# The token norm ahead of a quantized feed-forward: scale found after normalizing, steps moved between engines, batch 1's tokens spread over four tiles

## What is computed

```
x = x + attention(layernorm(x), ctx)
x = x + ffn(layernorm(x))            # this second layernorm, and what follows it

layernorm(x)  = (x - mean(x)) / sqrt(var(x) + 1e-5)
bit_linear(x, w, b):
    gamma_x = max(max(|x|), 1e-5);  scale_x = 127 / gamma_x         # per token
    x_dq = clip(round(x * scale_x), -128, 127) / scale_x
    gamma_w = max(mean(|w|), 1e-5)
    w_dq = clip(round(w / gamma_w), -1, 1) * gamma_w
    return x_dq @ w_dq.T + b
ffn(x) = bit_linear(silu(bit_linear(x, gate_w, gate_b)) * bit_linear(x, val_w, val_b), out_w, out_b)
```

## Time and profile before

| | |
|---|---|
| median of 3 runs | 970.87 us (970.19 to 971.57) |
| the profiled execution | 969.66 us, of which the trace's span is 967.6 us |
| PE busy over the span | 876.3 us (91%) |
| DVE / ACT / POOL busy | 834.3 / 528.2 / 556.3 us |
| last head's end to start of feed-forward | about 821 to 836.5 us |
| feed-forward | 836.5 us to the end |

### The profile page before, as it was taken

The page is one execution under the profiler, slowest core; times in us unless marked ns, Lnnn a source line. Parts: engine busy times, 40 slices in busy tenths (PEclk is TensorE's granted clock), DMA queues, the critical chain, the costliest instruction groups (busy, mean ns, idle before and its releaser), DMA issues. The chain is left out here.

```text
span 967.6 us, 15479 instructions
## 1 busy us (share of the span) xinstructions
PE 876.3 (91%) x4290; PEld 672.3 (69%) x4290; DVE 834.3 (86%) x1234; ACT 528.2 (55%) x885; POOL 556.3 (57%) x551
## 2 busy tenths in 40 slices
PE   3556999999999999999999999999999798738996
PEld 2434888878888788878888888888888676313543
DVE  6756899988998999899989988998899778686996
ACT  2315556655655575566656655665566477443332
POOL 5176646465555746574657465646464678664661
PEclk9768999999999999999999999999999998778999
DMA  8000121011101110111011101110210168100000
GB/s 302 0 21 27 55 67 36 27 40 47 46 14 50 46 35 24 39 46 35 24 39 46 35 24 44 50 39 20 66 46 14 34 252 306 52 0 12 22 22 33
DMA packets 25174, 51.73 MB, mean 53 GB/s; under 512 B 5440, under 2 KB 11840, under 8 KB 23872
## 3 DMA queue, kind: packets, MB, share of 16 engines
q1 hardware_dynamic: 24064, 49.36, 15.8%
q10 hardware_dynamic: 1088, 2.10, 0.6%
HBM read 49.35 MB, written 2.10 MB: 53 GB/s over the span
## 5 line engine op out<-in xcount | busy, mean ns | idle before, releaser
L791 POOL TENSOR_TENSOR rot_cos<-rot_cos,rot_sin 128x512 f32<-128x512 f32 x93 | 120.1, 1291 | 147.3 <-DVE rot_sin L985 135.7
L895 ACT ACTIVATE probs<-scores,neg_max 128x1024 f32<-128x1024 f32 x128 | 144.0, 1126 | 74.8 <-DVE neg_max L1011 74.0
L976 DVE TENSOR_TENSOR pt_lo<-banks,pt_hi 128x512 fp32r<-128x512 f32 x256 | 164.3, 683 | 9.8 <-ACT pt_hi L879 7.5
L879 ACT CAST pt_hi<-banks 128x512 fp32r<-128x512 f32 x256 | 138.3, 596 | 54.5 <-PE banks L1154 54.5
L1011 DVE TENSOR_REDUCE neg_max<-scores 128x1 f32<-128x1024 f32 x128 | 155.8, 1218 | 9.9 <-PE scores L1171 9.0
L1154 PE MATMUL banks<-ident,probs 128*128 128x128 f32 x1024 | 134.8, 275 | 10.0 <-PEq L1213 5.4
L1154 PEld LDWEIGHTS banks<-ident,probs 128*128 128x128 f32 x1024 | 119.9, 141 | 28.7 <-issue 5.8
L799 POOL TENSOR_TENSOR rot_lo<-rot_cos,rot_hi 128x512 fp32r<-128x512 f32 x93 | 119.7, 1287 | 7.8
L1006 DVE SCALAR_TENSOR_TENSOR acc<-banks,inv,acc 128x512 f32<-128x512 f32 x128 | 92.6, 747 | 12.9 <-PE banks L1086 10.9
L1086 PE MATMUL banks<-pt_hi,v_hi 128*128 128x512 f32 x256 | 102.9, 402 | 0.9
L1086 PE MATMUL banks<-pt_hi,v_lo 128*128 128x512 f32 x256 | 101.0, 394 | 0.0
(11 more groups left out here) (194 smaller groups left out, 2014.4 us busy)
## 6 DMA issues: line engine op xcount, KB each, us to landing
load<-in_pack SPq DMA_DIRECT2D x15, 320.0 KB, 2.9
raw_chunk<-in_out_w SPq DMA_DIRECT2D x8, 512.0 KB, 3.7
load<-in_pack SPq DMA_DIRECT2D x16, 256.0 KB, 2.7
raw_chunk<-in_gate_w SPq DMA_DIRECT2D x8, 512.0 KB, 3.6
raw_chunk<-in_val_w SPq DMA_DIRECT2D x8, 512.0 KB, 4.3
raw<-in_gate_w SPq DMA_DIRECT2D x4, 1024.0 KB, 5.8
raw<-in_val_w SPq DMA_DIRECT2D x4, 1024.0 KB, 5.1
raw<-in_out_w SPq DMA_DIRECT2D x4, 1024.0 KB, 5.2
```

Of the source, the lines that this page charges most:

```text
L791: nc.gpsimd.tensor_tensor(total, total, rot_sin[:, c, :], ALU.add).then_inc(rot_sum, 1)
L879: nc.scalar.copy(out, src).then_inc(group_hi, 1)
L895: nc.scalar.activation(probs[:, u % 2, :], scores[:, u % 2, :], ACT.Exp, bias=neg_max[:, u:u + 1], accum_out=sums[:, u:u + 1]).then_inc(ex ...
L976: return nc.vector.tensor_tensor(pair[1], src, pair[0].bitcast(F32), ALU.subtract)
```

## The change

- The last head and tiles 0 and 1: `statistics` is one DVE instruction per tile; maximum and minimum of the raw rows are gone. The rows are normalized without the quantization scale (`deviation`, `normalize`), and the largest magnitude is then taken from the normalized rows (`extreme`, one DVE pass per tile); `scales` has four small instructions.
- POOL's `lift` is two passes in place (times scale plus MAGIC; clip from both sides) over one buffer of four tiles, where it was one pass between two buffers of two.
- `take` moves from DVE to ACT. In the last head the transposes go to the `scores` banks.
- In the last head the second norm's steps stand ahead of V1's take-out on ACT and, partly, on DVE; two weight drops move behind them on ACT.
- In the feed-forward four tiles are written out, and batch 1's lifts, transposes and takes are placed in tiles 2 and 3 by three tables. Tiles 0 to 3 wait for their own token tile, the loop (tiles 4 to 7, two turns) for all eight.

```diff
+TOKENS_LIFTED = {(2, 0): 4, (2, 2): 5, (3, 0): 6, (3, 2): 7}
+TOKENS_TURNED = {(2, 7): 4, (3, 2): 5, (3, 5): 6, (3, 7): 7}
+TOKENS_TAKEN = {(3, 0): 4, (3, 1): 5, (3, 2): 6, (3, 3): 7}
...
     def statistics(self, dve, u):
-        nc, tile, one = self.nc, self.t["acc"][:, u, :], slice(u, u + 1)
-        nc.vector.bn_stats(self.stats[:, u, :], tile)
-        nc.vector.tensor_reduce(self.most[:, one], tile, AX, ALU.max)
-        nc.vector.tensor_reduce(self.least[:, one], tile, AX, ALU.min).then_inc(self.seen, 1)
+        self.nc.vector.bn_stats(self.stats[:, u, :], self.t["acc"][:, u, :]).then_inc(self.seen, 1)
...
+    def deviation(self, dve, b):
+        nc, half = self.nc, slice(b * U, (b + 1) * U)
+        rstd = self.rstd[:, half]
+        inverse_deviation(nc, dve, self.var_eps[:, half], self.root[:, half], rstd, self.tmp[:, half], self.root_ready, b + 1,
+                          lambda ins: self.link(dve, ins))
+        nc.vector.scalar_tensor_tensor(out=self.shift[:, half], in0=self.mv[:, half, 0], scalar=-1.0, in1=rstd, op0=ALU.mult,
+                                       op1=ALU.mult).then_inc(self.shift_ready, 1)
+
+    def normalize(self, act, u):
+        act.wait_ge(self.shift_ready, u // U + 1)
+        self.nc.scalar.activation(self.tile(u), self.t["acc"][:, u, :], ACT.Identity, bias=self.shift[:, u:u + 1],
+                                  scale=self.rstd[:, u:u + 1]).then_inc(self.normed_ready, 1)
+
+    def extreme(self, dve, u):
+        dve.wait_ge(self.normed_ready, u + 1)
+        self.nc.vector.tensor_reduce(self.most[:, u:u + 1], self.tile(u), AX, ALU.max,
+                                     apply_absolute_value=True).then_inc(self.most_ready, 1)
...
     def lift(self, pool, u):
-        pool.wait_ge(self.normed_ready, u + 1)
-        self.nc.gpsimd.tensor_scalar(self.lifted[:, u % 2, :], self.normed[:, u % 2, :], MAGIC, MAGIC + 127, ALU.add,
-                                     ALU.min).then_inc(self.lifted_ready, 1)
+        tile = self.tile(u)
+        pool.wait_ge(self.scale_ready, u // U + 1)
+        self.nc.gpsimd.tensor_scalar(tile, tile, self.x_scale[:, u:u + 1], MAGIC, ALU.mult, ALU.add).then_inc(self.lifted, 1)
+        pool.wait_ge(self.lifted, u + 1)
+        self.nc.gpsimd.tensor_scalar(tile, tile, MAGIC + 127, MAGIC - 128, ALU.min, ALU.max).then_inc(self.clipped, 1)
...
-    def take(self, dve, u, src):
-        return self.nc.vector.tensor_scalar(self.t["xt"][:, :, u * P:(u + 1) * P], src.rearrange("p (c s) -> p c s", c=KD),
-                                            MAGIC, -128.0, ALU.subtract, ALU.max)
+    def take(self, act, u, src):
+        act.wait_ge(self.turned, u + 1)
+        self.nc.scalar.activation(self.t["xt"][:, :, u * P:(u + 1) * P], src.rearrange("p (c s) -> p c s", c=KD),
+                                  ACT.Identity, bias=self.t["minus_magic"][:]).then_inc(self.taken, 1)
...
-            tile(Head(0), 0)
-            tile(Head(1), 1)
-            with engine.Fori(0, (NU - 2) // 2) as i:
+            for n in range(U):
+                tile(Head(n), min(n, 2))
+            with engine.Fori(0, (NU - U) // 2) as i:
...
-                if h.i is not None:
-                    pe.wait_ge(x_read, U)
+                if n == 0:
+                    pe.wait_ge(second.taken, h.number + 1 if h.i is None else NU)
...
+                pe.wait_ge(second.taken, u)
+                second.turn(pe, u, ps_x)
...
-                    if before == 1 and n == 1:
-                        second.scales(dve, 1)
-                    if before == 1 and n in (4, 6):
-                        take(U + n // 2 - 2)
-                    if before == 1 and n == NP - 1:
-                        take(NU - 2)
-                        take(NU - 1)
+                    if before == 1 and n == 3:
+                        second.deviation(dve, 1)
+                    if before == 1 and n >= NP - 2:
+                        second.extreme(dve, 2 * (n - NP + 2) + U)
+                        second.extreme(dve, 2 * (n - NP + 2) + U + 1)
+                    if h.i is None and h.number == 2 and n == 0:
+                        second.scales(dve, 1)
...
-                    if before == 1:
-                        second.normalize(act, U + n)
+                    if before == 1 and n:
+                        second.normalize(act, U + n - 1)
+                    if h.i is None and (h.number, n) in TOKENS_TAKEN:
+                        second.take(act, TOKENS_TAKEN[h.number, n], ps_x[:])
...
-                    if before == 1:
-                        lift(U + n)
+                    if h.i is None and (h.number, n) in TOKENS_LIFTED:
+                        second.lift(pool, TOKENS_LIFTED[h.number, n])
```

More of the change, by code:

```diff
@@ L66 @@
 A0, A1, V1, V0, C0, C1 = ("A", 0, "next"), ("A", 1, "next"), ("V", 1, "last"), ("V", 0), ("C", 0, "next"), ("C", 1, "next")
-UNGROUPED = ("score", "max", "exp", "sum", "double", "abs", "drop", "stats", "spread", "root", "scale", "norm")
+UNGROUPED = ("score", "max", "exp", "sum", "double", "abs", "drop", "stats", "spread", "root", "deviation", "norm", "extreme", "scale", "X", "take")
 PE_ORDER = (
@@ L114 @@
     ("T", 4, 1), ("T", 5, 0), ("exp", 6), ("drop", 5), ("T", 5, 1), ("exp", 7), ("T", 6, 0), ("T", 6, 1), ("T", 7, 0),
-    ("drop", 6), ("T", 7, 1), ("drop", 7), ("drop", 8), ("V", 1), ("root", 0), ("drop", 9), ("norm", 0), ("norm", 1),
-    ("norm", 2), ("norm", 3),
+    ("drop", 6), ("T", 7, 1), ("drop", 7), ("root", 0), ("norm", 0), ("norm", 1), ("V", 1), ("norm", 2), ("norm", 3),
+    ("drop", 8), ("drop", 9), ("take", 0), ("take", 1), ("take", 2), ("take", 3),
 )
@@ L534, in link, with spread @@
         dve.wait_ge(self.chain, self.links)
+    def spread(self, dve, b):
+        nc, half = self.nc, slice(b * U, (b + 1) * U)
+        dve.wait_ge(self.seen, U * (b + 1))
+        for u in range(b * U, (b + 1) * U):
+            ins = nc.vector.bn_aggr(self.mv[:, u, :], self.stats[:, u, :])
+        self.link(dve, ins)
+        nc.vector.tensor_scalar(self.var_eps[:, half], self.mv[:, half, 1], EPS, None, ALU.add).then_inc(self.var_ready, 1)
     def deviation_root(self, act, b):
@@ L564, in scales @@
[L564 to L568, removed]
+        x_gamma = t["x_gamma"][:, half]
+        dve.wait_ge(self.most_ready, U * (b + 1))
@@ L569, in scales @@
+        self.link(dve, nc.vector.tensor_scalar(x_gamma, self.most[:, half], 1e-5, 1.0 / 127.0, ALU.max, ALU.mult))
+        nc.vector.reciprocal(self.x_scale[:, half], x_gamma).then_inc(self.scale_ready, 1)
         for w, name in enumerate(("x_gate", "x_val")):
             nc.vector.tensor_scalar(t[name][:, half], x_gamma, t["gamma"][:, w:w + 1], None, ALU.mult)
[L572 to L578, removed]
@@ L933, in period @@
                         second.normalize(act, item[1])
+                    elif item[0] == "take":
+                        second.take(act, item[1], turned_tokens(item[1]))
                     else:
@@ L994, in take_out @@
                     return nc.vector.reciprocal(t["inv_gamma"][:], t["gamma"][:])
-                if kind == "X":
-                    dve.wait_ge(group_full, p.full(marked))
-                    return second.take(dve, group[1], src)
                 _, b, j = group
@@ L1146, in products @@
                     mm = three(out, [x[:, j * P:(j + 1) * P] for x in cv], [x[:] for x in m])
-                elif kind == "X":
-                    mm = second.turn(pe, group[1], out)
                 else:
@@ L1207, in period @@
                         products(p, item[3], item[1], item[2])
+                    elif item[0] == "X":
+                        second.turn(pe, item[1], turned_tokens(item[1]))
                     elif item[0] not in UNGROUPED:
@@ L1254, in _ @@
                 for u in range(U):
-                    if u >= 2:
-                        pool.wait_ge(group_full, Period(Head(H - 1), "last").full(("X", u - 2)))
                     second.lift(pool, u)
@@ L1592, in _ @@
         def _(pool):
-            def lift(u):
-                if u >= U + 2:
-                    pool.wait_ge(x_full, u - U - 1)
-                second.lift(pool, u)
             def add_bias(h):
@@ L1606, in tile @@
                     pool.wait_ge(out_bias_loaded, 16)
-                if h.number >= U or before == 2:
+                if h.i is not None:
                     pool.wait_ge(second.normed_ready, NU)
```

69 lines of the change are left out of this document (29 added, 40 removed), and 3 rows, old and new, of the table LAST_DVE.

## The result

| | median us | range, executions | ratio to before, 95% interval |
|---|---|---|---|
| before | 970.81 | 970.19 to 971.57, 4 | 1 |
| after | 955.05 | 950.62 to 956.12, 4 | 0.9829 [0.9802, 0.9856] |

The forecast was 957.4 us with a range of 952 to 963, so it was 2.35 us too high, and the range held.

A forecast was written before the change was run, and what follows sets the result against it. PE bounds the last 67.6 us; the change touches some 59 us before, where PE is not the bound. 0.85 + 18.2 - 5.6 = 13.5 us off 969.66 gives 956.2, plus 1.2 for the median: 957.4 us, range 952 to 963.

The forecast's parts named there:

- The handover, -0.85: From the last head to the feed-forward's start F: F comes 0.85 us earlier, though PE starts O1 2.5 us later.
- Tiles 0 and 1, -18.2: From F, the feed-forward's start, to the first contraction: 31.95 us instead of 50.2, bounds 28.4 and 35.
- its small steps are held by bias and product: Tile 1 on DVE: the range's small steps wait for POOL's bias and product, putting the scale at F + 19.0.
- half clock keep parts 3 and 4 back: Tile 0: PE at half clock delays parts 3 and 4, so the statistics end at F + 11.8, before 15.4.
- Tiles 2 and 3, +5.6: First contraction to tile 4: +1.6 us to the second contraction, then +4.0 for the last token.
- a PE wait of 2 to 3 us on ACT's take: Sign to look for: PE waits this long just ahead of tile 4.
- From there ... the same.: Tiles 4 to 7 and the end stay unchanged and PE-bound, at 11.26 us a tile.
- Rival 2: Tiles 2 and 3: batch 1's transposes wait on ACT and the clock falls once, 4 to 5 us more, 962 us; chance 0.15.
- Rival 1: Handover, tiles 0 and 1: held steps don't add up, first contraction at F + 28.4, 953 us; chance 0.17.
- Rival 3: POOL's new lift passes run at the old lift's 1.9 us each: 969 us, no change; chance 0.04.
- Rival 4: PE's granted clock stays at half through tiles 0 to 3, tile 4 at F + 77: 979 us; chance 0.04.

The follow-up runs named there:

- after_again: The changed kernel itself, unchanged, timed once more on another chip: 954.16 us, 0.9825 of before.
- clip_add_min: Changed kernel with the second lift pass on GpSimd doing plus 0 and minimum, lower clip left out: 963.15 us, 0.9936 of before.
- tokens_early: Changed kernel with batch 1's four tokens one to three slots earlier, all lifted in tile 2: 948.82 us, 0.9787 of before.
- tokens_early_again: Changed kernel with batch 1's four tokens one to three slots earlier, run again beside the unchanged changed kernel: 949.24 us, 0.9775 of before.
- lot9_later: Changed kernel with the last head's last weight lot on POOL moved into the feed-forward: 956.09 us, 0.9849 of before.
- old_steps_spread: Kernel before with its own steps, but four feed-forward tiles written out and batch 1's token work spread over tiles 1 to 3: 960.11 us, 0.9908 of before.

## Why the prediction was right

- **The handover, -0.85.** Measured -0.94 from the mark. Its parts held too: O1 at 827.08 for 826.45, the shift out at 824.16 for 823.4 (the two long steps shown above, which end with the POOL passes beside them), the first lift at 828.83 for 828.2; all three are late by no more than the mark is (0.8). That the size agrees to 0.1 us is luck: in `after_again`, with one hold less, the same handover gained 2.4 us. A lift goes from start to start in 1.49 us rather than 1.34, because its first pass takes 0.70 us for 0.62 and about 0.1 us lies between every two passes of POOL, where the sum had that once:

```profile
828.83 0.71 POOL L588 TENSOR_SCALAR normed_in_head<-normed_in_head,x_scale_second 128x512 f32<-128x512 f32 x1 [4.69 <-DVE x_scale_second L581]
...
830.33 0.70 POOL L588 TENSOR_SCALAR normed_in_head<-normed_in_head,x_scale_second 128x512 f32<-128x512 f32 x1
```

- **Tiles 0 and 1, -18.2.** Measured -20.6 (29.6 for 31.95). That small steps are held is right, but the terms were mis-sized, and one hold did not happen: "its small steps are held by bias and product" cost 2.3 us in the sum and 0.5 on the chip, what the steps take by themselves. DVE and the POOL instructions beside it, in tile 1 of after:

```profile
849.67 2.27 DVE L1472 TENSOR_REDUCE h_max<-hidden 128x1 f32<-128x2048 f32 x1
851.97 0.15 DVE L1475 TENSOR_SCALAR h_gamma<-h_max 128x1 f32<-128x1 f32 x1
852.16 0.21 DVE L1477 TENSOR_SCALAR h_out<-h_gamma,gamma 128x1 f32<-128x1 f32 x1
...
853.21 1.06 DVE L293 TENSOR_TENSOR tmp_second<-rstd_second 128x4 f32<-128x4 f32 x1
854.31 1.19 DVE L294 TENSOR_TENSOR tmp_second<-tmp_second,var_eps_second 128x4 f32<-128x4 f32 x1
```
```profile
851.76 1.26 POOL L1605 TENSOR_TENSOR acc<-acc,out_bias 128x512 f32<-128x512 f32 x1
852.99 2.49 POOL L1619 TENSOR_TENSOR hidden<-sigma,val 128x512 f32<-128x512 f32 x2
```

  The steps of 128x1 run in 0.15 and 0.21 us beside POOL's bias; two of those of 128x4 behind them are held, each to the end of a product (854.26 and 855.50), where the sum had one hold of 1.1. The account, by the sum's own marks: the range's large pass ends at F + 15.5 for 16.7 (-1.2), its small steps take 0.5 for 2.3 (-1.8), the shift's chain 3.1 for 2.25 (+0.8); so the chain is 2.2 us earlier, and the contraction with it. The first 1.2 us lie ahead of the range: the sum had half clock keep parts 3 and 4 back, and tile 0's statistics end at 11.8. In before the granted clock was full from F + 5.8. In the runs of the new steps the statistics end the sooner, the sooner it is full: at F + 11.0 with full clock from F + 4.5 (`clip_add_min`), 10.5 from F + 3.8 (after), 9.0 with full clock throughout (`after_again`). So this part of the forecast could only be right by chance.
- **Tiles 2 and 3, +5.6.** First contraction to tile 4 took 23.5 us for 22.85; before it was 17.35, so +6.1. The step from contraction to contraction was 12.5 us for 12.86. The last token cost more: tile 4 came 7.5 us behind the contraction's end for 6.6. It shows on POOL and ACT:

```profile
884.07 2.12 POOL L1619 TENSOR_TENSOR hidden<-sigma,val 128x512 f32<-128x512 f32 x1 [1.77 <-DVE val L1464]
886.17 0.69 POOL L588 TENSOR_SCALAR normed_in_ffn<-normed_in_ffn,x_scale_second 128x512 f32<-128x512 f32 x1
886.94 0.61 POOL L590 TENSOR_SCALAR normed_in_ffn<-normed_in_ffn 128x512 f32<-128x512 f32 x1
```
```profile
888.57 0.69 ACT L601 ACTIVATE xt<-ps_x,minus_magic 128x512 bf16<-128x512 f32 x1 [2.19 <-PE ps_x L595]
```

  The product is held by the rounding, as in the earlier trace rows, and ends 4.1 us behind the contraction for 3.8; the transposes take 0.83 for 0.5; the hand-overs are 0.2 longer. The 0.3 us of the product are a slip of the sum: it counted the 3.8 from the start of finish (913.04), but the 2.6 us of three groups from the contraction's end. In the same tile of before that end is the start of the next group, and the product ends 4.1 us behind it, as in after:

```profile
912.72 4.48 PE L1385 MATMUL ps_gv<-ternary,xt 128*128 128x512 bf16 x20
```

  The sign "a PE wait of 2 to 3 us on ACT's take" came as two waits, and the longer one is on POOL's clip.
- **"From there ... the same."** Not quite. With the 3.3 us of waits ahead of tile 4 the clock fell to half from 888.0 to 894.8. From tile 4 to the loop's last contraction after took 50.5 us (889.5 to 939.97), before 47.8 (904.1 to 951.94), so 2.6 us were lost there. Rival 2 had one fall of the clock in it, and that much of it came. 1.3 us of it were given back at the very end: the last contraction ran at full clock in after's profile and partly at half in before's, where the granted clock was 0.50 to 0.60 from 959 to 962 (the last rows of each, before first). That is chance: it took 3.62 us in `tokens_early` and 4.82 in `tokens_early_again`, one and the same kernel.

```profile
959.79 4.62 PE L1433 MATMUL ps_o<-ternary,ht 128*128 128x512 bf16 x16
```
```profile
947.46 3.62 PE L1442 MATMUL ps_o<-ternary,ht 128*128 128x512 bf16 x16
```

- **Terms that were off, together.** -2.35 in tile 1, +0.6 in tiles 2 and 3, +1.3 from tile 4 on, +0.8 ahead of the mark (which lies between 771.93 and 773.00 in the traces of the versions of after, 772.15 in before), -0.1 in the handover, -0.2 outside the span (1.82 us for 2.06). These cancel, and so the profiled execution came out at 956.12 for 956.2; that is luck. A second execution of the same kernel shows how good a single term is, some 1.5 us:

| us | before | after | after_again |
|---|---|---|---|
| mark to F | 64.40 | 63.46 | 61.96 |
| F to the first contraction | 50.2 | 29.6 | 29.0 |
| first contraction to tile 4 | 17.35 | 23.5 | 24.6 |
| tile 4 to the end | 63.5 | 64.8 | 63.9 |

  The median of after is 1.1 us below its profiled execution, where 1.2 above had been added by before's; that is nearly all of the 2.35 us of miss.
- **The rivals.** Rival 1's 953 is as near to the measured 955.05 as the forecast's 957.4, so the time does not choose between them; the traces do. Rival 1 was right in that the 128x1 steps go free and nearer in size for the first contraction (28.4 against 31.95, measured 29.6 and 29.0), and wrong in that the others do not: holds of 1.85, 1.74, 1.06 and 1.19 us are in after. Rival 3 falls: the new passes took 0.61 to 0.71, and `clip_add_min` shows what would have brought it. (Its own terms, 9 and 2.5 us, add up to 970 rather than 969.) Rival 4 falls: the clock was at half until 840.2 and again from 857 to 861, and 0.96 in tiles 2 and 3.

The Trainium skill (SBUF — State Buffer, "Who interferes with whom") has a `tensor_scalar` in a 2-port mode contend with GpSimd. The 128x4 steps and the rounding behaved so (1.85 us, 2.28 us); the 128x1 `tensor_scalar` steps, whose input and output are in SBUF as well, did not (0.15 us), in after, in `lot9_later` and in `old_steps_spread`. Which condition lets them out no run here separates.

## What to carry to other kernels

When a chain of small VectorE steps sits beside a GpSimd pass, price each step by what GpSimd is running at that moment and by its width, and expect that moving the pass may only move the hold and that the number of holds changes from one execution to the next, by 1.5 us here. When work is spread thin to free one stretch, look for the last piece of it: here it was the lift behind the last product, and placing the four lifts up to three products earlier won 5 us. Two halves of a change that clear the same stretch don't add up; run each alone before crediting either. And when a forecast is right to 0.1 us on one execution, look at a second one before trusting its terms.

## What had not been expected of the hardware

- A GpSimd `tensor_scalar` on 128x512 takes 1.93 us with plus and minimum, 0.61 with minimum and maximum, 0.69 with times and plus.
- VectorE `tensor_scalar` steps on 128x1 took 0.15 to 0.21 us beside a GpSimd pass, those on 128x4 up to 1.85 us. The same chain had two long holds in one execution and one in another, as the GpSimd pass began 0.3 us later.
- Ahead of tile 4 PE waited 2.3 and 1.0 us within some 5 us, after 19 us (866.3 to 885.2) with hardly a wait. A stretch of 7 us at 0.51 followed in one execution, at 0.76 in another. In six profiles with such waits the clock fell there, in four without them it stayed at 1.00.
